# A click-prediction tower with 39 embedding fields on one core: another order of its SBUF buffers

## What is computed

```python
x0 = xk = e                      # e: [512, 39, 16], gathered rows
for W in (f0, f1, f2):           # [39*39, 128], [128*39, 128], [128*39, 128]
    z = einsum('bfd,bgd->bfgd', x0, xk).reshape(b, f * g, d)
    xk = einsum('bpd,pm->bmd', z, W)
    outs.append(xk)
z = concatenate(outs, axis=1).sum(-1)          # [512, 384]
h = relu(concatenate([z, dense_ctx], 1) @ W_top1 + b_top1)
h = relu(h @ W_top2 + b_top2)
y = h @ W_top3
```

## Time and profile before

| | |
|---|---|
| median of 3 runs | 654.74 us (654.56 to 655.45) |
| the profiled execution | 655.72 us |
| its span, first to last instruction | 653.8 us |
| instructions | 10942 |
| TensorE busy | 623.2 us, 3102 matmuls |
| VectorE busy | 525.0 us |
| ScalarE busy | 337.7 us |
| GpSimd busy | 501.8 us |
| moved by DMA | 43.40 MB |

### The profile page before, as it was taken

One profiled execution on the slowest core, in us unless ns is written; L12 is line 12 of the kernel. 1 busy time (PEld: TensorE's weight loads), 2 busy tenths in 40 slices (PEclk: granted clock), 3 DMA queues, 4 the chain that ended last, 5 costly groups with the idle time before them and its releaser, 6 DMA issues.

```text
span 653.8 us, 10942 instructions
## 1 busy us (share of the span) xinstructions
PE 623.2 (95%) x3102; PEld 468.0 (72%) x3102; DVE 525.0 (80%) x1651; ACT 337.7 (52%) x1148; POOL 501.8 (77%) x486
## 2 busy tenths in 40 slices
PE   0599999999999999999999999999999999999998
PEld 0476777777796777777787777777787777778763
DVE  4499989989857898989867798989876798988800
ACT  3153646465543646565553556555553555557602
POOL 6789989898957889898975888898985786566710
PEclk9999999999999999999999999999999999999999
DMA  6464038231305013140404014040403104000000
GB/s 225 97 169 124 15 85 293 43 93 28 109 4 131 4 30 106 12 125 8 128 4 117 18 11 126 8 128 3 133 4 96 39 6 129 1 1 2 1 1 0
DMA packets 59014, 43.40 MB, mean 66 GB/s; under 512 B 37648, under 2 KB 42926, under 8 KB 58826
## 3 DMA queue, kind: packets, MB, share of 16 engines
q1 hardware_dynamic: 52854, 38.00, 20.0%
q0 software_dynamic: 5120, 1.32, 2.5%
q10 hardware_dynamic: 980, 3.39, 1.5%
HBM read 40.75 MB, written 1.94 MB: 65 GB/s over the span
## 4 chain that ended last, share of the span: by engine, by line
PE 90%; DMA 3%; DVE 2%; POOL 1%; SPq 1%; issue 1%; ACT 1%; POOLq 0%; DVEq 0%; ACTq 0%
PE strip L795 22%; PE strip L799 21%; PE strip L796 21%; PE acc L755 14%; PE acc L827 4%; PE strip L813 2%; DVE scaled L582 1%; PE strip L827 1%; PE strip L893 1%; PE acc L764 1%; DVE z L537 1%; DMA found<-in_tables,rows 1%; ACT first L687 1%; POOL found L467 1%; DMA shifted<-x_fields 0%
## 5 line engine op out<-in xcount | busy, mean ns | idle before, releaser
L582 DVE SCALAR_TENSOR_TENSOR scaled<-strip,x_t,scaled 128x128 f32<-128x128 f32 x1216 | 331.8, 340 | 26.8 <-PE strip L799 25.8
L795 PE MATMUL strip<-w_hi,x_hi 128*128 128x512 f32 (+1 forms) x640 | 298.3, 466 | 0.8 <-ACT x_hi L631 0.7
L799 PE MATMUL strip<-w_hi,x_lo 128*128 128x512 f32 (+1 forms) x640 | 248.9, 389 | 0.0
L796 PE MATMUL strip<-w_lo,x_hi 128*128 128x512 f32 (+1 forms) x640 | 248.4, 388 | 0.0
L477 POOL TENSOR_TENSOR added<-added,product 128x512 f32<-128x512 f32 x128 | 171.2, 1338 | 74.3 <-ACT product L687 71.3
L687 ACT ACTIVATE product<-strip,x_t 128x128 f32<-128x128 f32 x512 | 146.6, 372 | 144.1 <-PE strip L799 144.1
L467 POOL DMA_INDIRECT found<-in_tables,rows x160 | 160.7, 1004 | 28.5 <-issue 10.9
L795 PEld LDWEIGHTS strip<-w_hi,x_hi 128*128 128x128 f32 x640 | 120.2, 188 | 49.0 <-issue 15.0
L796 PEld LDWEIGHTS strip<-w_lo,x_hi 128*128 128x128 f32 x640 | 120.5, 188 | 44.9 <-issue 25.3
L799 PEld LDWEIGHTS strip<-w_hi,x_lo 128*128 128x128 f32 x640 | 120.1, 188 | 25.7
L687 ACT ACTIVATE added<-strip,x_t 128x128 f32<-128x128 f32 x256 | 73.0, 367 | 91.7 <-PE strip L799 91.7
(11 more groups left out here) (57 smaller groups left out, 181.7 us busy)
## 6 DMA issues: line engine op xcount, KB each, us to landing
shifted<-x_fields SPq DMA_DIRECT2D x105, 234.0 KB
x_thrice<-x_fields SPq DMA_DIRECT2D x15, 234.0 KB
found<-in_tables,rows POOLq DMA_INDIRECT x160, 5.0
w<-in_L_rec_f SPq DMA_DIRECT2D x1, 2496.0 KB, 10.4
g_sum<-in_L_rec_f ACTq DMA_DIRECT2D x4, 512.0 KB, 7.9
shifted<-x_half_fields SPq DMA_DIRECT2D x14, 117.0 KB
x_once<-x_fields SPq DMA_DIRECT2D x15, 78.0 KB
x_fields<-found SPq DMA_DIRECT2D x15, 72.0 KB
```

Source lines behind the costliest of these rows:

```text
L582: dve.scalar_tensor_tensor(into, strip[:, slot_of_strip(q) % Y_BANKS, j, :], x0_t[:, c % 2, s, f:f + 1], onto, ALU.mult, ALU.add).then_inc ...
L795: pe.matmul(into, x1_hi[:, c % 2, columns], hi, start=True, stop=False)
L796: pe.matmul(into, x1_hi[:, c % 2, columns], lo, start=False, stop=False)
L799: pe.matmul(into, x1_lo[:, c % 2, columns], hi, start=False, stop=True).then_inc(strip_ready, 1)
```

## The change

Only the order of the `sb(...)` calls changes, and one buffer is added, `spare`, of 96 words of a partition (384 bytes), which nothing reads or writes.

```diff
-        ident = sb("ident", [P, P])
-        mask = sb("mask", [P, TILE_B])
+        sb("spare", [P, 3 * P // 4])
+        ident = sb("ident", [P, P])
         w0 = sb("w0", [ROWS, T0, MAPS])
         w1_hi = sb("w1_hi", [P, FIELDS, MAPS], F32R)
         w1_lo = sb("w1_lo", [P, FIELDS, MAPS], F32R)
         w2 = sb("w2", [P, FIELDS, MAPS])
-        ids = sb("ids_sb", [P, CHUNKS + 2, GATHERS], I32)
-        rows = sb("rows", [P, CHUNKS, GATHERS], I32)
-        found = sb("found", [P, E_SLOTS, GATHERS, D])
         x0_thrice = sb("x0_thrice", [ROWS, 2, N])
...
         x1_lo = sb("x1_lo", [MAPS, 2, N], F32R)
-        x0_t = sb("x0_t", [P, 2, SUBS, FIELDS])
-        x0_diag = sb("x0_diag", [P, SUBS, TILE_B, FG])
         first = sb("first", [P, 2, PER_STRIP, MAPS])
...
         out2 = sb("out2", [MAPS, BATCH])
-        dense = sb("dense_sb", [P, QUARTERS, D])
         dense_t = sb("dense_t", [P, BATCH])
-        bias1 = sb("bias1", [P, H1 // P])
-        bias2 = sb("bias2", [P, H2 // P])
         wt1 = sb("wt1", [P, 3, H1])
         wt1_dense = sb("wt1_dense", [P, H1])
         wt2 = sb("wt2", [P, H1 // P, H2])
+        mask = sb("mask", [P, TILE_B])
+        ids = sb("ids_sb", [P, CHUNKS + 2, GATHERS], I32)
+        rows = sb("rows", [P, CHUNKS, GATHERS], I32)
+        found = sb("found", [P, E_SLOTS, GATHERS, D])
+        x0_t = sb("x0_t", [P, 2, SUBS, FIELDS])
+        x0_diag = sb("x0_diag", [P, SUBS, TILE_B, FG])
+        dense = sb("dense_sb", [P, QUARTERS, D])
+        bias1 = sb("bias1", [P, H1 // P])
+        bias2 = sb("bias2", [P, H2 // P])
         wt3 = sb("wt3", [P, H2 // P])
```

## The result

The changed kernel takes 653.47 us, the median of 17 runs (652.56 to 655.16), against 655.61 for the kernel before in as many runs (654.56 to 656.83). The ratio is 0.997, its 95% interval 0.9961 to 0.9979: 1.4 to 2.6 us less. That is small, but the interval clears the 0.2% (a ratio of 0.998) that the prediction took as the least that a measurement can tell, if only just. The forecast was 654.7 and its range held the time; its likeliest case, no change, was not what happened. The profiled execution took 652.78 us with a span of 651.0, against 655.72 and 653.8.

The account below looks back on a forecast made before the run. TensorE's matmul spacing was taken to bound the kernel from 80 us on; the profiled 655.7 us plus four terms of 0 gave 655.7, and the runs' median, 1 us lower, made the forecast 654.7, range 650 to 662.

Parts of the forecast that it names:

- likeliest case: Whole kernel: no change in time, own range 653.5 to 656 us, chance 0.66.
- What bounds the kernel: Whole span: from 80 us on, number of matmuls times their spacing; before that loads, gathers and VectorE.
- Step (a): Strip matmuls streaming w1 at new addresses: spacing unchanged, 0; bounds at most 34 us to gain, 14 us to lose.
- strips get quicker: Strip matmuls: w1 off the 64-byte grid slows them; all excess gone gives 621 to 626 us; chance 0.20.
- partial case: Strip matmuls: one eighth to one third of the excess goes, giving 643 to 651 us; chance 0.08.
- strips get slower: Strip matmuls: reading w1 while loading x1 at the same offset clashes, giving 662 to 669 us; chance 0.11.
- Step (b): Stationary operands x1_hi and x1_lo: each load of 188 ns is covered by a matmul of 232, cost 0.
- Step (c): ScalarE and VectorE operations: durations unchanged, 0; VectorE has 2.39 us to spare in a chunk.
- Step (d): DMA into SBUF at the start: taken as 0; at most a fraction of 5.5 us either way.

Follow-up runs that it names:

- the shortened kernel before: The kernel before with VectorE's 1472 scaled additions done on 112 of the 128 columns: 667.61 us on another chip, ratio 0.9979.
- (160, 384): Strip matmuls alone, moving operand 160 and stationary 384 bytes past a multiple of 512, as in the kernel before: 0.2325 us each.
- the first run: The whole computation left out, only strip matmuls on 32 listed pairs of moving and stationary offsets, no other engine at work: spacings from 226.8 to 234.4 ns.

## Why the prediction was right in part and wrong in its main case

- **What bounds the kernel** held in the main: TensorE from 80 us on, with the strips' spacing as the one number that an address could move. The whole effect was in that number. But "TensorE has no slack" was not the whole of it: the shortened kernel before has mostly chunks of 34.93 instead of 35.13 us, so up to 0.2 us of a chunk were VectorE's even before.
- **Step (a), "I take 0", is the step that failed.** The spacing fell by 3.5 ns. I had compared two alignments by the float32 matmuls, L885 and L888 against L893. Those still take 0.4293 us an entry in the changed kernel, where both of their operands lie at one offset, so they would have shown nothing under any of the theories; and the comparison was of one operand's offset to a grid, when it is the offset between two operands that counts. The bounds held: 6.0 us of TensorE's time lies between the 14 to lose and the 34 to gain, though the lower end of the spacing, 0.2147, was reached by no pair.
- **That the time fell inside the range is in part luck.** The range went down to 650 for a partial gain, priced as if TensorE's saving were passed on almost in full. The 6.0 us so passed on would have given 654.7 - 6.0 = 648.7, below the range. Two errors worked against each other: a gain taken as 0, and a wait for VectorE that was left out.
- **The rival "strips get quicker"** had the place and the sign, with 0.20, but argued from the moving operand's own offset, which the runs with only the weights moved disproved. Its partial case was priced at 4 to 12 us; one fifth of the excess went (3.5 of 17.8 ns), and more than half of that was not passed on. Its counter-argument, that a start which is off costs once per matmul, fits no better: at (160, 384) the excess was 10, 14 and 18 ns with 256, 384 and 512 columns.
- **The rival "strips get slower"** named the right pair, stationary and moving at one offset, and drew the opposite conclusion: that is the quick case. It was taken as a clash for which no row spoke.
- **Step (b)**, stationary operands at cost 0, looked only at whether a load is covered (188 under 232 ns). It is covered, and still its address matters.
- **Step (c)** held in durations: 339 and 341 ns for the scaled additions, 687 for both forms of ScalarE's. But its 2.39 us of slack for VectorE in a chunk was a sum of idle time, not room for TensorE to come earlier. With 0.38 us to give, 0.10 arrived, and only with VectorE's columns cut did 0.34 arrive.
- **Step (d)**: on the chain at the start, the transfer of `shifted` took 3.61 us after and 3.02 before, and one of `x_once` 2.25 and 2.52 (not the same half of the first chunk). They show no gain, and the first strip came at 28.78 us against 28.47. The packets of 2048 bytes, most of the traffic, took a median of 84 ns both 128 past a multiple of 256 and on it, so the 6% that step (d) priced did not come. The 512 packets of 4096 bytes that bring the raw weights into `g_sum` did shrink, from 168 ns (96 past a multiple of 256) to 159 (on it); they take 159 to 162 in the other whole kernels that have `g_sum` on a multiple of 512, and 167 to 168 in those that have it where it was. None of it shows in the time.
- **The figure of the skill's page** for the spacing of matmuls (the Trainium skill, "TensorE: Matmul & The Clock Gate", section "Wait — 56ns, not 53.3ns?"), 215.7 ns, is reached by no pair of offsets: the best is 226.8. The Trainium skill's page "SBUF — State Buffer" (section "Who interferes with whom") says that TensorE has two read ports, one for the moving and one for the stationary operand, which are independent. No run here looks at the ports; what the runs show is that the offset of the two operands to each other changes the spacing by 6 ns alone and 3.5 in the kernel.

What stays open: why equal offsets modulo 256 help at 128 stationary and 512 moving columns, why so little with 384 and not at all with 256, why another offset is quicker with 64 stationary columns, why the quick spacing comes only some matmuls after an interruption, and what the remaining 12 ns are.

## What to carry to other kernels

Look at the distance from start to start of the matmuls that carry the time, and compare it with the best form in the same trace; if it is some per cent longer, try the offset of the stationary operand to the moving one, with two pads, before aligning everything. Expect the gain in long unbroken runs of one shape; here it was there in full only from about the tenth matmul on. A saving on the engine that fills the span is passed on only as far as the next engine can follow, and the idle share of that engine does not tell how far: a run that leaves out a little of its work does. The same holds in the other direction: work moved to an engine with idle time costs what waits behind its last instruction.

## What the runs showed of the hardware

- A float32r matmul of 512 columns with 128 stationary ones follows the last one after 227 to 229 ns where both operands begin at the same offset modulo 256 bytes of a partition, after 229 with the moving one 64 ahead and 231.5 with it 16 ahead, and after 232 to 234 ns at the 21 other pairs of the first run; no other engine has to be at work.
- In the kernel the quick spacing of 226.8 ns is reached from about the tenth matmul after a float32 or a narrower one; the first three take 232.
- Alignment of either operand to 32, 64 or 512 bytes by itself has no effect on that spacing: (32, 32) and (160, 160) are as quick as (256, 256).
- With 384 moving columns that gain is within the scatter, with 256 it is a loss of 2. With 512 moving columns the spacing does not fall with a smaller stationary operand: at equal offsets it is 230 ns with 64 columns and 231.5 with 32. With 256 moving ones it does, from 119.4 to 114.1 ns with 64 columns.
- Activations of ScalarE (687 to 688 ns, 128x512) and scaled additions of VectorE (339 to 344 ns) did not follow the offsets of their operands; 342 to 344 stand in the three kernels that ran with only one group moved, also where the additions' own operands lay as before.
- Packets of 4096 bytes into SBUF took a median of 168 ns at 96 past a multiple of 256 bytes and 159 on one; packets of 2048 bytes took 84 at 128 past and on it.
